# The second attention of layer two: constants by DMA between POOL's products, an earlier weight load, four staging halves

## The reference, cut to what matters

```python
qkv = hidden_states @ qkv_w + qkv_b
q, k, v = jnp.split(qkv, 3, axis=-1)          # 32 heads x 16 columns
q = _rope(q, cos, sin); k = _rope(k, cos, sin)  # x1*cos - x2*sin, x2*cos + x1*sin
scores = jnp.einsum('bqhd,bkhd->bhqk', q, k) * scale
scores = scores + (1.0 - causal) * MASK_VAL
probs = jax.nn.softmax(scores, axis=-1)
ctx = jnp.einsum('bhqk,bkhd->bqhd', probs, v).reshape(b, s, e)
return ctx @ out_w + out_b
```

## Time and profile before

| what | us |
|---|---|
| median of 3 runs | 2263.75 (2261.89 to 2265.6) |
| the profiled execution, its own time | 2262.22 |
| its span in the trace | 2259.0 |
| mean granted TensorE clock | 0.954 of full |
| TensorE busy | 2068.7 (92%) |
| VectorE (DVE) busy | 1391.4 (62%) |
| ScalarE (ACT) busy | 1164.2 (52%) |
| GpSimd (POOL) busy | 828.4 (37%) |

### The profile page before, as it was taken

The page is one execution under the profiler, slowest core; times in us unless marked ns, Lnnn a source line. Parts: engine busy times, 40 slices in busy tenths (PEclk is TensorE's granted clock), DMA queues, the critical chain, the costliest instruction groups (busy, mean ns, idle before and its releaser), DMA issues. The chain is left out here.

```text
span 2259.0 us, 33216 instructions
## 1 busy us (share of the span) xinstructions
PE 2068.7 (92%) x11536; PEld 1480.2 (66%) x11536; DVE 1391.4 (62%) x2513; ACT 1164.2 (52%) x2691; POOL 828.4 (37%) x1000
## 2 busy tenths in 40 slices
PE   5999987999999999999988689999999985899988
PEld 3333355777888888888766567777777674754457
DVE  5888564535666666666646456666666565567756
ACT  4677543245655655655534455555555433335553
POOL 0000100235545545545430145554455313537611
PEclk8999978999999999999999799999999986989999
DMA  3000012671112021021011334433443102743301
GB/s 117 1 1 1 5 71 78 186 242 38 33 53 66 24 62 56 30 66 47 20 38 49 106 92 112 111 90 99 113 96 88 37 24 69 183 80 73 71 24 38
DMA packets 95538, 157.68 MB, mean 70 GB/s; under 512 B 11967, under 2 KB 33471, under 8 KB 93198
## 3 DMA queue, kind: packets, MB, share of 16 engines
q1 hardware_dynamic: 85774, 134.19, 21.1%
q0 software_dynamic: 9600, 21.38, 3.7%
HBM read 90.51 MB, written 31.46 MB: 54 GB/s over the span
## 5 line engine op out<-in xcount | busy, mean ns | idle before, releaser
L2528 POOL TENSOR_TENSOR attn1a_probs<-attn1a_probs,attn1a_recip 128x128 f32<-128x128 f32 (+3 forms) x256 | 178.9, 720 | 232.7 <-DVE attn1a_recip L2711 232.0
L1889 POOL TENSOR_TENSOR attn0b_probs<-attn0b_probs,attn0b_recip 128x128 f32<-128x128 f32 (+3 forms) x256 | 196.0, 787 | 185.3 <-DVE attn0b_recip L2133 185.2
L2584 ACT ACTIVATE attn1a_probs<-attn1a_scores,attn1a_negmax 128x128 f32<-128x128 f32 (+3 forms) x256 | 132.7, 523 | 174.0 <-DVE attn1a_negmax L2697 172.8
L1993 ACT ACTIVATE attn0b_probs<-attn0b_scores,attn0b_negmax 128x128 f32<-128x128 f32 (+3 forms) x256 | 132.8, 524 | 122.4 <-DVE attn0b_negmax L2126 121.8
L1440 DVE TENSOR_REDUCE attn0a_negmax<-attn0a_by_query 128x2 f32<-128x1024 f32 x128 | 151.9, 1219 | 10.2 <-PE attn0a_by_query L1557 10.2
L2697 DVE TENSOR_REDUCE attn1a_negmax<-attn1a_scores 128x2 f32<-128x256 f32 (+3 forms) x128 | 105.4, 824 | 70.0 <-PE attn1a_scores L2886 70.0
L1882 POOL TENSOR_TENSOR attn0b_q_cos<-attn0b_q_cos,attn0b_q_swap 128x512 f32<-128x512 f32 x64 | 84.2, 1315 | 159.6 <-DVE attn0b_q_swap L2115 159.6
L2001 ACT ACTIVATE attn0b_probsT_hi<-attn0b_turned 128x256 fp32r<-128x256 f32 (+3 forms) x128 | 90.1, 704 | 88.5 <-PE attn0b_turned L2277 86.9
L2126 DVE TENSOR_REDUCE attn0b_negmax<-attn0b_scores 128x2 f32<-128x256 f32 (+3 forms) x128 | 105.0, 820 | 46.9 <-PE attn0b_scores L2266 46.9
L2898 PE MATMUL attn1a_turned<-ident_f,attn1a_probs 128*128 128x128 f32 x640 | 115.6, 279 | 8.8 <-DVE attn1a_probsT L2705 7.4
L2112 DVE TENSOR_TENSOR attn0b_q_cos<-attn0b_aux,attn0b_cos_q 128x512 f32<-128x512 f32 x60 | 41.5, 692 | 115.9 <-ACT attn0b_q_swap L2014 115.9
(11 more groups left out here) (516 smaller groups left out, 6217.9 us busy)
## 6 DMA issues: line engine op xcount, KB each, us to landing
pre<-in_b_o SPq DMA_DIRECT2D x16, 1024.0 KB, 5.4
attn1a_qT<-attn1a_stage SPq DMA_DIRECT2D x128, 128.0 KB, 2.4
attn1a_qT<-attn1a_stage SPq DMA_DIRECT2D x64, 256.0 KB, 3.8
attn0b_vals<-attn0b_v_out SPq DMA_DIRECT2D x16, 512.0 KB, 4.0
attn0b_keys<-attn0b_part SPq DMA_DIRECT2D x32, 256.0 KB, 4.2
pre<-in_b_q SPq DMA_DIRECT2D x8, 1024.0 KB, 7.7
attn0b_kT<-attn0b_keys SPq DMA_DIRECT2D x64, 128.0 KB, 2.8
pre<-in_b_kv SPq DMA_DIRECT2D x5, 1024.0 KB, 6.4
```

What stands on the lines that cost most here:

```text
L1889: pool.tensor_tensor(x, x, recip[:, r % DEEP, e:e + 1].broadcast_to([P, (qt + 1) * P]), ALU.mult).then_inc(s_scaled, 1)
L1993: act.activation(probs[:, r % DEEP, e, 0:width], scores[r % 2][:, e, 0:width], ACT.Exp, bias=negmax[:, r % 2, e:e + 1], accum_out=sums[:, ...
L2528: pool.tensor_tensor(x, x, recip[:, r % DEEP, e:e + 1].broadcast_to([P, (qt + 1) * P]), ALU.mult).then_inc(s_scaled, 1)
L2584: act.activation(probs[:, r % DEEP, e, 0:width], scores[r % 2][:, e, 0:width], ACT.Exp, bias=negmax[:, r % 2, e:e + 1], accum_out=sums[:, ...
```

## The change

- POOL's six copies of zeros and the six DMA issues behind them go. The constant rows of all six mix buffers, zeros of the queries' included, are loaded by twelve DMAs of 64 KB from a DRAM constant that now has a part for each kind, one issued behind each of POOL's sine products 1 to 12.
- POOL's first low half of the value weights moves from behind product 9 to behind product 10, the second is at 11 as before.
- SP issues the load of the value weights behind `spread_out(4)`, where it was behind `spread_out(6)`.
- The staging halves of `part_hi` and `part_lo` become four each, with four semaphores, so a split waits for the stores of k - 4.

```diff
-    RAWS = 4
-    SPLIT_SECOND, SPLIT_THIRD, SPLIT_THIRD_LO = (1, 2, 4, 6), (9, 10, 11, 12), (9, 11, 13, 14)
+    RAWS, PARTS = 4, 4
+    SPLIT_SECOND, SPLIT_THIRD, SPLIT_THIRD_LO = (1, 2, 4, 6), (9, 10, 11, 12), (10, 11, 13, 14)
...
-            part_hi, part_lo = take_sb("part_hi", [P, 2, SEQ], F32R), take_sb("part_lo", [P, 2, SEQ], F32R)
+            part_hi, part_lo = take_sb("part_hi", [P, PARTS, SEQ], F32R), take_sb("part_lo", [P, PARTS, SEQ], F32R)
...
-        s_spread = [n.sem("spread_even"), n.sem("spread_odd")]
+        s_spread = [n.sem(f"spread{k}") for k in range(PARTS)]
...
-                sp.dma_start(into[:, at:at + HD // 2, :], part_hi[:, i % 2, :].bitcast(F32)).then_inc(s_spread[i % 2], 16)
+                sp.dma_start(into[:, at:at + HD // 2, :], part_hi[:, i % PARTS, :].bitcast(F32)).then_inc(s_spread[i % PARTS], 16)
...
-                if i == SPLIT_SECOND[-1]:
+                if i == SPLIT_SECOND[-1] - 2:
                     load_weights(2)
...
-            for mix in (k_mix, q_mix):
-                for i in range(3):
-                    pool.tensor_copy(mix[:, i, :, :].rearrange("p a x -> p (a x)"),
-                                     negmax[:, :, :, :, :].rearrange("p s t e x -> p (s t e x)")).then_inc(s_zero, 1)
-            pool.wait_ge(s_zero, 9)
-            for e in range(2):
-                for i in range(3):
-                    pool.dma_start(k_mix[ROWS * e + USED:ROWS * (e + 1), i, :, :], d["c1_ones"]).then_inc(s_ones, 16)
+
+            constants = [(mix, kind, e, buffer) for kind, mix in enumerate((k_mix, q_mix)) for e in range(2)
+                         for buffer in range(3)]
+
+            def load_constants(mix, kind, e, buffer):
+                pool.dma_start(mix[ROWS * e + USED:ROWS * (e + 1), buffer, :, :], d["c1_ones"][kind]).then_inc(s_ones, 16)
...
                     split_value_weights(SPLIT_THIRD_LO.index(i))
-            pool.wait_ge(s_ones, 96)
+                if 1 <= i <= len(constants):
+                    load_constants(*constants[i - 1])
+            pool.wait_ge(s_ones, 16 * 12)
             for written in s_spread:
-                pool.wait_ge(written, 16 * 2 * (NB // 2))
+                pool.wait_ge(written, 16 * 2 * (NB // PARTS))
...
-                if k >= 2:
-                    act.wait_ge(s_spread[k % 2], 16 * 2 * (k // 2))
-                act.activation(part_hi[:, k % 2, :], turned[turned_block(k) % 4], ACT.Copy).then_inc(s_hi, 1)
+                if k >= PARTS:
+                    act.wait_ge(s_spread[k % PARTS], 16 * 2 * (k // PARTS))
+                act.activation(part_hi[:, k % PARTS, :], turned[turned_block(k) % 4], ACT.Copy).then_inc(s_hi, 1)
...
-            pe.wait_ge(s_zero, 9)
+            pe.wait_ge(s_zero, 3)
...
-    ones = np.zeros((16, 2, SEQ), np.float32)
-    ones[0, 0], ones[1, 1] = 1.0, 1.0
+    ones = np.zeros((2, 16, 2, SEQ), np.float32)
+    ones[0, 0, 0], ones[0, 1, 1] = 1.0, 1.0
```

More of the change, by code:

```diff
@@ L3040, in spread_out @@
                 sp.wait_ge(s_hi, i + 1)
-                sp.dma_start(into[:, at:at + HD // 2, :], part_hi[:, i % 2, :].bitcast(F32)).then_inc(s_spread[i % 2], 16)
+                sp.dma_start(into[:, at:at + HD // 2, :], part_hi[:, i % PARTS, :].bitcast(F32)).then_inc(s_spread[i % PARTS], 16)
                 sp.wait_ge(s_lo, i + 1)
-                sp.dma_start(into[:, HD + at:HD + at + HD // 2, :], part_lo[:, i % 2, :].bitcast(F32)).then_inc(
-                    s_spread[i % 2], 16)
+                sp.dma_start(into[:, HD + at:HD + at + HD // 2, :], part_lo[:, i % PARTS, :].bitcast(F32)).then_inc(
+                    s_spread[i % PARTS], 16)
             load_weights(1)
@@ L3219, in split @@
                 dve.wait_ge(s_hi, k + 1)
-                if k >= 2:
-                    dve.wait_ge(s_spread[k % 2], 16 * 2 * (k // 2))
-                dve.tensor_tensor(part_lo[:, k % 2, :], turned[turned_block(k) % 4], part_hi[:, k % 2, :].bitcast(F32),
+                if k >= PARTS:
+                    dve.wait_ge(s_spread[k % PARTS], 16 * 2 * (k // PARTS))
+                dve.tensor_tensor(part_lo[:, k % PARTS, :], turned[turned_block(k) % 4], part_hi[:, k % PARTS, :].bitcast(F32),
                                   ALU.subtract).then_inc(s_lo, 1)
```

## The result

| | before | changed |
|---|---|---|
| median, us | 2263.75 | 2249.33 |
| lowest and highest of 5 runs | 2261.89, 2267.89 | 2246.17, 2253.59 |
| ratio of the run times, 95% interval | | 0.9941 [0.9925, 0.9956] |
| the profiled execution, its span | 2259.0 | 2250.6 |
| from the first projection matmul to the first score | 86.53 | 69.98 |

What follows compares the result with a forecast made beforehand. Three TensorE gaps in the opening of layer two's second attention, with low clock behind each, cost 16.85 us. Removing 6.22 + 4.60 + 5.9 = 16.7 us takes the median 2263.75 to 2247.0; range 2244.0 to 2252.0.

Steps and rivals of the forecast that it cites:

- Gap A: TensorE's wait ahead of block 4, from POOL's late start: 4.59 us plus 1.63 slow pace; all 6.22 goes.
- Gap B: TensorE's wait ahead of block 12, for the value weights' load: 2.95 us plus 1.65 slow pace; all 4.60 goes.
- Gap C: TensorE's wait ahead of the third value block, for staging: 3.07 us plus 2.96 slow pace; 5.9 of 6.03 goes.
- The low clock: TensorE falls to 1.2 GHz after idling about 3 us, adding 1.63, 1.65 and 2.96 us behind the opening's three gaps.
- rival 1: Last low half or first values up to 1 us late, clock falls again: 12.7 us gained, 2251; chance 0.11.
- POOL's issues: Twelve issues of constants behind products 1 to 12, 0.50 to 0.63 us each, charged at nothing.
- the cover: POOL's product and issue, 1.74 us, fit an ordinary block's 2.80; 0.2 late at blocks 10 and 11, caught up at 12.
- the formula: POOL's issues at cost c a block hold TensorE by 12 (c - 1.56) + 2.48 us; slower rival, chance 0.02.
- The mixes: Mixes must be loaded before the first scores; spare time falls from 10.5 to 6.4 us.
- Behind the first scores: Scoring and everything after moves as one, no change taken; low-clock stretch bounded at 2.5 us either way.

Runs made afterwards that it cites:

- the kernel with all but the fills' part: The kernel before with the early load and four staging halves, but POOL's copies and issues of constants left as they were; opening 76.05 us.
- the changed kernel's second profile: The changed kernel profiled again with nothing altered; opening 69.82 us, started at 1902.09, no gaps of TensorE.

## Why the prediction was right, point by point

- **Gap A, 6.22 us.** Right in cause and size. Product 0 started 6.02 us after the first matmul (5.8 were worked out), and the kernel with all but the fills' part is 76.05 - 69.98 = 6.07 us longer.
- **Gap B, 4.60 us.** Gone as forecast, but two things in the step were off. I took 6.40 us for the landing; it took 7.10, 8.3 in the changed kernel's second profile and up to 8.7 in the other kernels with this edit, so the spare time was 0.35 to 1.95 us and not 2.65. The limit itself, 9.05 us from issue to landing, was right: counted from the first matmul, behind the sixth store the load was issued 4.19 us later and was rounded 6.88 behind its issue, and 4.19 + 6.88 less the gap of 1.97 is 9.1. And I gave the four halves no part in B. The early load alone leaves 1.51 us, the early load with two halves 0.55, both with ACT standing for stores; with four halves nothing. What I charged at nothing, that the megabyte slows the stores beside it, was real, and the other edit paid for it. That B went whole is in part luck: I had not seen that it needed the four halves, and they were in the change for another reason.
- **Gap C, 5.9 us.** Right for the wait: the first values followed the last low half at 0.60 us, as worked out, and no gap is left ahead of block 18. Only the 2.96 us of low clock in this term are less sure than the 3.07 of the gap, as the next point shows.
- **The low clock.** Right as a sum for these two kernels, wrong as a price of each gap. I tied 1.6 to 3.0 us to each; behind gaps of 3.06 to 3.08 us at C it cost 0.11 in three kernels and 2.88 in one (2.96 by the slightly faster pace of the values, as I reckoned it). So single parts can't be added up, and my argument against rival 1, that the low clock followed only gaps of about 3 us, does not hold: it also came behind gaps of 1.97 and 2.10 us. The close match of 16.7 and 16.55 is partly built in, since both are read from the same profile of the kernel before. Had C's excess been 0.11 us in that profile, as it was three times out of four, the stage would have shown some 13.8 us. What goes in any case is the 4.59 + 2.95 + 3.07 = 10.6 us of gaps.
- **POOL's issues.** 0.55 us, within 0.50 to 0.63; the cover held. At 2.04 us of issuing a block the gaps sum to 6.8 us, where the formula gives 8.2 less the slack at the start. That POOL's first low half moved from product 9 to 10 was never run by itself; the kernel with the early load and four halves kept it at 9 and shows no gap but A, so no part of the 16.55 us is shown to be its.
- **The mixes.** 5.7 us spare, 6.4 forecast.
- **Behind the first scores.** Unchanged, 275.08 against 275.17. The bound of 2.5 us either way held: 273.87 to 277.60 over the ten profiles whose scoring is the same, which is 1.3 below to 2.4 above the 275.17.
- **The total.** 2247.0 forecast, 2249.33 and 2249.01 measured. The working gives 16.7, the stage gave 16.55 and, in the second profile, 16.71. In the profiled execution of the first measurement, what is missing lies ahead of the opening; for the medians no stage is known. In fourteen profiles the same code starts the opening anywhere from 1897.26 to 1907.33; the changed kernel and those built on it start it from 1897.59 to 1905.54. Nothing ties the late starts to the change. I had put 3.0 us into the range for clock and spread together, which is too little beside a 10 us spread of a single execution; the medians stayed within it.

## What to carry to other kernels

Read each gap for the one instruction queued in front of the one that is waited for, and work out its new start from rows; that gave the gap at A to within 0.2 us and left none at B and C. Price the gap and the low clock behind it apart, since the gap came back to within 0.4 us from kernel to kernel and the low clock did not. Edits that each remove a gap can still need each other, so ask what a transfer moved earlier will run beside, and give its neighbours' landing times a bound of their own. Compare kernels by stage, since a change of 16 us was shown as 8 by two whole executions.

## What the runs showed of the hardware

- The granted clock does not follow a gap's length alone. TensorE ran at full pace behind gaps of 3.06, 3.07 and 3.08 us and at the low level behind 3.07 us in the kernel before; behind 1.97 us it fell 1.0 us after TensorE was at work again and stayed down for eight intervals; behind the gaps of 0.55 to 1.75 us in the table it never fell. The Trainium skill (TensorE: Matmul & The Clock Gate, "What's actually happening") says that the activity is watched on a clock of its own that doesn't start with the kernel; the scatter here agrees with that.
- Fourteen profiled executions of the same code ahead of the opening differ by 10 us; the three that start the opening latest are those in which TensorE stands at 0.50 to 0.51 from 1320 to 1330 us, at the head of an attention.
- A 1 MB load among 256 KB stores landed in 6.4 to 8.7 us for the same bytes, and the low-half stores issued just behind it in 5.0 to 6.4 where the median store of the kernel before took 2.8 us.
- A DMA issue on POOL takes 0.51 us for 16 KB and 0.50 for 64 KB when several are issued back to back, and 0.55 for a single one of 64 KB between products: the count of issues is the price, not the bytes.
